# Upward products of the first expert layer: five full-array passes against four and a paired half-array pass

## What is computed

```python
def _mlp(x, wg, wu, wd):
    return jax.nn.silu(x @ wg) * (x @ wu) @ wd
xf = x.reshape(-1, h)                       # 756 x 192, after a layernorm
shared = _mlp(xf, sw_gate, sw_up, sw_down)  # 192 -> 384 -> 192
...
for e in range(E):                          # E = 7
    out = out + cw[:, e:e + 1] * _mlp(xf, rw_gate[e], rw_up[e], rw_down[e])
```

## Time and profile before

| what | value |
|---|---|
| median of 3 runs | 634.9 us (634.78 to 635.33) |
| the profiled execution | 640.5 us, its span in the profile 638.7 us |
| TensorE (PE) busy | 564.8 us, 88% of the span |
| VectorE, ScalarE, GpSimd busy | 41%, 33%, 17% |
| first expert layer | about 206.8 to 338 us of the span |

### The profile page before, as it was taken

How to read it: one execution, slowest core, us unless ns; L and a number is a source line. 1 busy time by engine, 2 the same in 40 slices (tenths; PEclk the granted TensorE clock), 3 DMA queues, 4 the chain that set the end, 5 groups by cost and what they waited for, 6 DMA issues and landing times.

```text
span 638.7 us, 9285 instructions
## 1 busy us (share of the span) xinstructions
PE 564.8 (88%) x3321; PEld 503.3 (79%) x3321; DVE 261.5 (41%) x758; ACT 212.3 (33%) x529; POOL 106.2 (17%) x104
## 2 busy tenths in 40 slices
PE   6999899999899999999999785999999964599990
PEld 5768889576889999999997685868977854499990
DVE  1731924165673333333335975334344445122112
ACT  3041523223714444444423423355356220011220
POOL 0020000020002222121210000016005330672221
PEclk9886958668996999999999796855875675599996
DMA  8950000000000122222231100000000040164424
GB/s 271 258 122 1 2 1 0 1 1 1 1 1 19 62 89 92 92 92 92 92 111 37 38 1 0 1 2 0 1 0 0 1 142 5 32 182 136 151 60 116
DMA packets 19772, 36.82 MB, mean 58 GB/s; under 512 B 6581, under 2 KB 13828, under 8 KB 18718
## 3 DMA queue, kind: packets, MB, share of 16 engines
q1 hardware_dynamic: 17182, 34.49, 17.7%
q0 software_dynamic: 2560, 1.93, 1.2%
HBM read 32.75 MB, written 4.07 MB: 58 GB/s over the span
## 4 chain that ended last, share of the span: by engine, by line
PE 55%; issue 25%; DVE 10%; POOL 5%; DMA 2%; ACT 2%; SPq 0%; POOLq 0%; ACTq 0%; DVEq 0%
PE bank L426 34%; PE bank L767 4%; POOL wB L1621 4%; PE bank L756 3%; PE bank L753 3%; PE bank L512 1%; PE bank L754 1%; PE bank L750 1%; PE bank L779 1%; PE bank L444 1%; DMA big<-yd 1%; DVE lg L1377 1%; ACT xT L989 1%; DVE big L1367 1%; PE bank L554 1%
## 5 line engine op out<-in xcount | busy, mean ns | idle before, releaser
L426 PE MATMUL bank<-raw,big 128*126 128x192 f32 (+1 forms) x480 | 79.9, 326 | 0.0
L426 PEld LDWEIGHTS bank<-raw,big 128*126 128x126 f32 (+1 forms) x480 | 78.2, 178 | 0.0
L426 PE MATMUL bank<-xS,wA 128*128 128x378 f32 x288 | 66.6, 339 | 0.5 <-POOL wB L1621 0.5
L1351 DVE TENSOR_TENSOR big<-bank,big 128x378 f32<-128x378 f32 x48 | 26.5, 552 | 66.8 <-PE bank L426 47.6
L1621 POOL TENSOR_TENSOR wB<-raw,wA 128x768 fp32r<-128x768 f32 x16 | 28.7, 1815 | 148.6 <-ACT wA L950 148.6
L426 PEld LDWEIGHTS bank<-xS,wA 128*128 128x128 f32 x288 | 51.1, 189 | 1.4 <-issue 1.4
L426 PE MATMUL bank<-xS,wB 128*128 128x378 f32 x192 | 48.8, 335 | 0.0
L956 ACT ACTIVATE big<-bank 128x378 f32<-128x378 f32 x48 | 23.2, 487 | 63.1 <-PE bank L426 63.1
L431 PE MATMUL bank<-ident 128*128 128x128 f32 x266 | 37.2, 307 | 4.7 <-ACT lg L973 4.0
L431 PEld LDWEIGHTS bank<-ident 128*128 128x128 f32 x266 | 36.5, 223 | 5.6 <-ACT lg L973 4.5
L426 PE MATMUL bank<-big,raw 96*128 96x190 f32 x192 | 34.5, 342 | 2.4 <-issue 2.4
(11 more groups left out here) (374 smaller groups left out, 1063.9 us busy)
## 6 DMA issues: line engine op xcount, KB each, us to landing
raw<-in_fgu SPq DMA_DIRECT2D x8, 1152.0 KB, 5.1
raw<-in_mfc SPq DMA_DIRECT2D x8, 576.0 KB
raw<-in_mpj SPq DMA_DIRECT2D x8, 576.0 KB, 4.6
big<-in_w SPq DMA_DIRECT2D x5, 576.0 KB, 7.0
raw<-in_fdn SPq DMA_DIRECT2D x8, 288.0 KB, 5.2
big<-in_p SPq DMA_DIRECT2D x3, 432.0 KB, 4.8
yd<-big SPq DMA_DIRECT2D x1, 1134.0 KB
xd<-xn SPq DMA_DIRECT2D x2, 567.0 KB
```

The source lines that it names most:

```text
L426: mm = te.matmul(o, l, r, start=first and k == 0, stop=last and k == len(pairs) - 1)
L1351: ve.tensor_tensor(aT[s][:, m, u * HALF:(u + 1) * HALF], ps[:, 0:HALF], sg[:, 3 * u + m, :], ALU.mult).then_inc(emptied_v, 1)
```

## The change

The 64 input rows that do not fill a chunk are arranged so that they stand in both halves of the partitions, and the low weights of these 64 rows are no longer multiplied in a full-array pass:

- The weights' chunks become rows 0-127, rows 128-191 twice, and rows 0-127 (line 1715 before). `cat` becomes the 192 high columns, the low columns 128-191, the low columns 0-127: VectorE's one subtraction becomes two.
- `xS` gets a fourth chunk, transposed from columns 64 to 191 of `cat`, whose rows 64-127 are the high part of features 128-191. So there are four transposes for each of the six token tiles where there were three, and ScalarE's copy has 504 columns instead of 378.
- For each pair of groups (gate and up of one `u` and `m`) both banks are taken first. Then come two products of 64 rows: the gate's on rows 0-63 of `wB` chunk 1 with `xS` chunk 1, the up's on rows 64-127 of `wB` chunk 1 with `xS` chunk 3, each of 128 output rows into its own bank. Then come four full passes for the gate and four for the up: three with `wA`, one with `wB` chunk 0.
- To make room for the fourth chunk, `e32` and `r1T` no longer have storage of their own, they use `h1` and `vB`.

```diff
-        xS = sb("xS", [128, 3, T], F32R)
+        xS = sb("xS", [128, 4, T], F32R)
...
-        e32 = sb("e32", [B * 9, D])
...
-        h1 = sb("h1", [TT, NT, D]); h2 = sb("h2", [TT, NT, D])
+        h1 = sb("h1", [TT, NT, D]); e32 = h1[0:B * 9, 0, :]; h2 = sb("h2", [TT, NT, D])
...
-        rw1 = sb("rw1", [DH + 1, 2, 16]); r1T = sb("r1T", [16, T]); rw2 = sb("rw2", [16, 3]); rb2 = sb("rb2", [TT, 3])
+        rw1 = sb("rw1", [DH + 1, 2, 16]); r1T = vB[0:16, :]; rw2 = sb("rw2", [16, 3]); rb2 = sb("rb2", [TT, 3])
...
-                for c in range(3):
-                    mm = te.transpose(ps[:, c * TT:(c + 1) * TT], cat[:, t, c * 128:(c + 1) * 128], ident[0:TT, 0:TT])
+                for c, c0 in enumerate((0, 128, 256, 64)):
+                    mm = te.transpose(ps[:, c * TT:(c + 1) * TT], cat[:, t, c0:c0 + 128], ident[0:TT, 0:TT])
...
-                            for z, nm_ in enumerate("gu"):
-                                n = slice(z * FI + m * 128, z * FI + (m + 1) * 128)
-                                acc(take((nm_, s, u, m), i)[:, 0:HALF],
-                                    [(wA[:, c, n], xS[:, c, cs]) for c in range(3)] + [(wB[:, c, n], xS[:, c, cs]) for c in range(2)]
-                                    ).then_inc(bank_full, 1)
+                            out_ = [take((nm_, s, u, m), i)[:, 0:HALF] for nm_ in "gu"]
+                            n = [slice(z * FI + m * 128, z * FI + (m + 1) * 128) for z in range(2)]
+                            for z, rows in enumerate((slice(0, 64), slice(64, 128))):
+                                te.matmul(out_[z], wB[rows, 1, n[z]], xS[rows, 1 + 2 * z, cs], start=True, stop=False)
+                            for z in range(2):
+                                acc(out_[z], [(wA[:, c, n[z]], xS[:, c, cs]) for c in range(3)] + [(wB[:, 0, n[z]], xS[:, 0, cs])],
+                                    first=False).then_inc(bank_full, 1)
...
-                ac.activation(xS[:, :, t * TT:(t + 1) * TT], ps[:, 0:3 * TT].rearrange("p (c t) -> p c t", c=3), ACT.Copy).then_inc(emptied_s, 1)
+                ac.activation(xS[:, :, t * TT:(t + 1) * TT], ps[:, 0:4 * TT].rearrange("p (c t) -> p c t", c=4), ACT.Copy).then_inc(emptied_s, 1)
...
-            ve.tensor_tensor(cat[:, :, D:2 * D], xn[:, :, :], cat[:, :, 0:D], ALU.subtract).then_inc(cat_r, 1)
+            st(ve.tensor_tensor(cat[:, :, D:256], xn[:, :, 128:D], cat[:, :, 128:D], ALU.subtract))
+            ve.tensor_tensor(cat[:, :, 256:2 * D], xn[:, :, 0:128], cat[:, :, 0:128], ALU.subtract).then_inc(cat_r, 1)
...
-    put("fgu", np.concatenate([gu, gu], 1).reshape(FE, 3, 128, 2 * FI).swapaxes(1, 2).reshape(FE, 128, 6 * FI))
+    put("fgu", np.concatenate([gu[:, 0:128], gu[:, 128:], gu[:, 128:], gu[:, 0:128]], 1).reshape(FE, 3, 128, 2 * FI).swapaxes(1, 2).reshape(FE, 128, 6 * FI))
```

## The result

The changed kernel took 649.2 us (median of four runs, 647.9 to 654.5) against 635.1 us for the kernel before (four runs, 634.8 to 641.5): a ratio of 1.0214, 95% interval 1.0161 to 1.0266. The forecast was 646.7 us in a range of 636 to 656. The profiled execution took 654.5 us, its span is 652.6.

A forecast was written before the change was run, and what follows sets the result against it. TensorE's passes in the expert layer's upward product were taken as the bound; 48 steps x 0.218 = +10.5 us, plus 1.3 us ahead of the loop, gave +11.8 on 634.9: 646.7 us, range 636 to 656.

The forecast's parts named there:

- The turn, +0.092 and +0.104 us: Expert loop on TensorE: each switch between full and 64-row passes costs a 0.092 us drain and a 0.104 us exposed weight load.
- The halves run together: Expert loop: a pair of 64-row products costs one full pass, 0.174 us, with 0.348 us as the other end.
- Hidden loads: Rival, chance 0.07: weight loads at turns are hidden behind the pass before, a step costs +0.01 us, total 636.7 us.
- free turns: Rival, chance 0.10: turns in the loop cost nothing, each step saves 0.174 us, total 627.8 us.
- Serial halves: Rival, chance 0.05: the two 64-row products do not run together, another 8.4 us, total 655.1 us.
- The clock: Rival, chance 0.04: the loop with its turns no longer holds 2.4 GHz, 80 us or more, total over 715 us.
- Ahead of the loop, +1.3 us: Before the expert loop: 24 transposes instead of 18 cost 1.25 us, plus 0.1 or so for the last longer copy.
- Storage: The new places of two buffers add no instruction and no wait: nothing.
- earlier wait for the up bank: Expert loop: the up bank is asked for 0.87 us earlier but was emptied long since: nothing.
- VectorE's second piece: Ahead of the loop: the subtraction in two pieces ends some 0.1 us later, while TensorE is with the router: nothing.
- the 0.9 us that GpSimd has to spare: Expert loop: GpSimd ends `wB` 0.9 us before the downward product's last matmul, so it does not bound.

The follow-up runs named there:

- r5_onehalf: The changed kernel with both 64-row products of a step on rows 0 to 63, one behind the other: 659.0 us median, ratio 1.0411.
- r6_apart: The changed kernel with each step's two 64-row products apart, each before its own four full passes: 672.8 us median, ratio 1.0618.
- r1_storage: The kernel before with only the change's storage: room for a fourth chunk, not written, and two buffers in their new places: 636.2 us median, ratio 1.0014.
- a2_change: The changed kernel run once more, in another group of runs: 649.2 us median, ratio 1.0258.
- r2_prep: The changed kernel with the old loop of ten full passes per pair of groups, keeping storage and 24 transposes: 639.6 us median, ratio 1.0026.
- r3_loop: The kernel before with only the change's loop, three chunks in `xS`, the up's 64-row product reading chunk 1: 646.2 us median, ratio 1.0181.
- r7_threeloop: The kernel before with only the loop of `r4_three`, its up 64-row products reading chunk 1: 639.4 us median, ratio 1.0018.
- r4_three: The changed kernel with the 64-row products of three pairs of groups put together, 16 visits instead of 48: 641.9 us median, ratio 1.0102.
- r4b_three: The kernel `r4_three` run a second time, beside `r7_threeloop`: 641.0 us median, ratio 1.0079.
- r8_early3: `r4_three` with the first expert's weight cast before the copies to `xS`, later casts behind the SiLUs, no spin: 632.4 us median, ratio 0.9946.
- r9_early: The kernel before with the early cast and no spin of `r8_early3`, loop of ten full passes: 632.4 us median, ratio 0.9907.

## Why the prediction was right

**The turn, +0.092 and +0.104 us, was right, and it is nearly the whole result.** It was read off other lines of the kernel before (751 to 753, 426 to 718, 488 to 426). Measured in the changed kernel: 0.26 us from full pass to pair and 0.37 to the next full pass, predicted 0.25 and 0.37; a step 1.95 us, predicted 1.96. Over 16, 48 and 96 visits the price is the same, 0.193 to 0.194 us a turn. The loop grew by 10.3 us, predicted 10.5. The exposed load is seen as such; that the other 0.09 us is the emptying of the array is the prediction's reading, and no run takes it apart.

**The halves run together**, as line 523 does: shown by `r5_onehalf`, 8.0 us.

**The rivals.** Hidden loads and free turns are ruled out by each turn in the trace. Serial halves are ruled out by `r5_onehalf`. The clock was 1.00 through the loop, even with 96 visits (`r6_apart`, 203.6 to 366.1).

**Ahead of the loop, +1.3 us, right in size and wrong in its path.** The step that failed: "The spin begins when the copies are done, and the loop behind it". In the profile I had, the spin ended last; in every later one with a spin the clock rose early and the loop waited for ScalarE's casts and GpSimd's low parts. Both chains start at the same copies, so the 1.2 us pass through either way. I read the "1.4 us before the loop starts" of `wB` as slack that lasts, and it was the late clock of that one execution. In the comparison of the two first profiles the two effects cancel to 0.0, so this term was not in the pair of profiles that the forecast spoke of; that later pairs have 1.1 to 1.4 us is in part luck, since the path was another.

**Storage, earlier wait for the up bank, VectorE's second piece: nothing.** `r1_storage` shows the first. For the second, the only waits before the 64-row products that last beyond a turn are for `wB`. The third ends 2.5 us before the first transpose. One reading was too wide: the 0.9 us that GpSimd has to spare hold for every second expert, while three of the others wait for `wB`, before and after alike, so the difference is not touched.

**The missing 2.2 us.** 11.8 were forecast; the first comparison gave 14.0, `a2_change` 11.4 on the means and 2.6% by its ratio. What changed code explains is 10.3 + 1.2 = 11.5. The rest of the first comparison lies in stretches whose code is the same, 4.6 us longer ahead and 0.9 shorter behind. The same changed kernel reached its first transpose at 199.60 us in one profile and at 191.19 in the other, so such differences come without any edit.

All the runs together show what this is, since each has its mean granted clock beside its time. The clock has two levels, so the span times twice what the mean lacks to 1 is the time spent at 1.2 GHz. Over the 69 runs of the kernel before in the three groups, a line through these points rises by 0.29 us for each us at 1.2 GHz, and single runs lie 1.6 us from it (standard deviation). Taking that line's share off every run leaves the difference that a kernel has at equal time at 1.2 GHz. "By its stretches" is what its profile has more than `r1_storage`'s from the first transpose to the loop's last product:

| kernel | us at 1.2 GHz, mean | by its stretches | at equal time at 1.2 GHz |
|---|---|---|---|
| before | 215 | | 0 |
| the change, first comparison | 222 | +11.6 | +11.1 |
| `a2_change` | 217 | +11.4 | +11.2 |
| `r2_prep` | 219 | +1.3 | +1.3 |
| `r3_loop` | 213 | +10.2 | +9.4 |
| `r5_onehalf` | 224 | +19.4 | +19.4 |
| `r6_apart` | 212 | +38.2 | +38.0 |
| `r7_threeloop` | 224 | -2.1 | -1.8 |
| `r4_three` | 231 | -0.8 | +0.2 |
| `r4b_three` | 230 | -0.7 | -0.2 |
| `r8_early3` | 226 | -7.5 | -7.7 |
| `r9_early` | 219 | -4.9 | -7.0 |

The last column is good to about 1 us. `r1_storage` stands at -0.5. `r9_early`'s stretches hold 2.0 us that its first passes lose at 1.2 GHz, which the last column takes off. So both comparisons of the change agree at 11 us, the grouped loop does bring its 2 us, and nearly all that `r4_three` and `r4b_three` lose against their loops is 15 us more at 1.2 GHz, some 4.4 us of time. Whether the edit causes that, no run shows.

## What to carry to other kernels

A 64-row product next to full ones is not half a pass. Count the visits to the smaller tile first, each with some 0.09 us between the two sizes and one bare weight load on the way in and again on the way out (here 2 x 0.194 us against 0.174 saved), and put as many small products into one visit as there are free banks (six were tried). Price it from a place in the same trace where the tile size changes, by the distance of starts: busy shares and recorded lengths hide it. And before a saving of two or three microseconds is believed, look at how far the kernel's own runs lie apart (10 to 18 us within one group here, where the prediction held 1.3 us to be the least that can be told), and compare runs at equal time at the lower clock.

## What the runs showed of the hardware

Runs of one and the same kernel before lay between 630 and 648 us on three chips, while its loop is 125.5 us at full clock in all three profiles that hold it (the kernel before, `r1_storage`, `r2_prep`). With the same instructions, the attention stretch took 76.7 us (`r1_storage`) to 85.6 (`r4_three`) from its first to its last mask product, in step with the mean clock: four profiles have 76.7 to 77.3 us at 0.64 to 0.65, six 78.7 to 79.4 at 0.62 to 0.63, two 82.4 at 0.60, and one 85.6 at 0.58.

```profile
404.20:481.30 77.10, 77.10 (x445) 59.97 (x443) 32.31 (x97) 40.21 (x185) 17.33 (x20) 0.65 0.00 1
```

is `r1_storage`, 77.1 us at 0.65, beside the 86.0 us at 0.58 of `r4_three` above. The two kernels with the grouped loop and the longer stretch ahead had long ones in all three of their profiles (85.6, 82.4 and, in `r8_early3`, 82.4 us). Whether a kernel's own timing steers the clock of a later stage is open.
